# Last head and low-rank stage: row variance from a Gram matrix, and one output chunk through ScalarE and GpSimd

## What is computed

```python
Bx = jnp.einsum('bni,bri->bnr', x, B[adapter_ids])      # rank 16
out = jnp.einsum('bnr,bor->bno', Bx, A[adapter_ids])    # back to 512
mu = jnp.mean(out, -1); var = jnp.mean(jnp.square(out - mu), -1)
h = (out - mu) * jax.lax.rsqrt(var + EPS) * gamma + beta
h = dyn_quant_linear(h, w1, b1); h = gelu(h); h = dyn_quant_linear(h, w3, b3)
x = x + h
```

## Time and profile before

| | us |
|---|---|
| median of 3 runs | 570.07 (569.52 to 570.65) |
| the profiled execution, its own time | 569.7 |
| span of that execution in the trace | 567.9 |
| TensorE busy | 542.2 |
| VectorE busy | 485.0 |
| ScalarE busy | 363.0 |
| GpSimd busy | 400.2 |

### The profile page before, as it was taken

One profiled execution on the slowest core, in us unless ns is written; L12 is line 12 of the kernel. 1 busy time (PEld: TensorE's weight loads), 2 busy tenths in 40 slices (PEclk: granted clock), 3 DMA queues, 4 the chain that ended last, 5 costly groups with the idle time before them and its releaser, 6 DMA issues.

```text
span 567.9 us, 10485 instructions
## 1 busy us (share of the span) xinstructions
PE 542.2 (95%) x3135; PEld 425.0 (75%) x3139; DVE 485.0 (85%) x626; ACT 363.0 (64%) x940; POOL 400.2 (70%) x410
## 2 busy tenths in 40 slices
PE   6999989999999999999999999999999999987885
PEld 3555768888888888888888888888888888865432
DVE  3553859997999799979997999799979998976897
ACT  3573567657665766576657665766576656665895
POOL 3005577799779977997799779977997799851063
PEclk9999999999999999999999999999999999999999
DMA  8752435422442244124512451245124312200003
GB/s 289 180 123 76 123 88 160 113 56 58 137 124 51 62 133 126 43 65 133 128 37 66 134 132 33 61 136 136 34 61 135 97 34 61 80 1 1 1 20 129
DMA packets 38172, 51.93 MB, mean 91 GB/s; under 512 B 12100, under 2 KB 20452, under 8 KB 38148
## 3 DMA queue, kind: packets, MB, share of 16 engines
q1 hardware_dynamic: 35652, 46.94, 31.3%
q10 hardware_dynamic: 2016, 3.48, 1.9%
q0 software_dynamic: 480, 1.22, 0.7%
HBM read 28.55 MB, written 2.10 MB: 54 GB/s over the span
## 4 chain that ended last, share of the span: by engine, by line
PE 80%; DVE 10%; issue 3%; DMA 2%; ACT 2%; POOL 2%; ACTq 0%; SPq 0%; DVEq 0%; POOLq 0%
PE pair L1378 23%; PE pair L1379 23%; PE flow L1367 9%; PE flow L1494 9%; PE flow L1486 4%; PE pair L1315 4%; DVE y_max L1191 2%; DVE raw_v L1081 1%; PE flow L1372 1%; DMA stage<-in_x 1%; PE flow L1315 1%; DMA swap_q<-raw_q 1%; DVE rope_c L1203 1%; DVE ctx_lo L1102 1%; DVE probs L1203 1%
## 5 line engine op out<-in xcount | busy, mean ns | idle before, releaser
L1095 DVE SCALAR_TENSOR_TENSOR accT<-pair,so_now,accT 128x1024 f32<-128x1024 f32 x125 | 157.2, 1274 | 14.8 <-PE pair L1379 13.9
L1081 DVE SCALAR_TENSOR_TENSOR raw_q<-pair,sc_now,raw_q 128x1024 f32<-128x1024 f32 x90 | 115.4, 1283 | 6.2 <-ACT raw_q L777 2.8
L560 POOL TENSOR_TENSOR probs<-probs,rowinv 128x512 f32<-128x512 f32 x64 | 66.8, 1044 | 65.4 <-DVE rowinv L1068 65.4
L722 ACT ACTIVATE probs<-flow,negmax 128x128 f32<-128x128 f32 x248 | 87.6, 369 | 32.8 <-DVE negmax L1049 32.8
L1378 PE MATMUL pair<-ctx_hi,wo 128*128 128x512 f32 x256 | 104.9, 410 | 2.8 <-issue 1.5
L1378 PE MATMUL pair<-h_hi,wq 128*128 128x512 f32 x240 | 100.0, 417 | 0.3 <-ACT raw_q L777 0.3
L1379 PE MATMUL pair<-ctx_lo,wo 128*128 128x512 f32 x256 | 100.2, 392 | 0.0
L1379 PE MATMUL pair<-h_lo,wq 128*128 128x512 f32 x240 | 94.1, 392 | 0.0
L529 POOL TENSOR_TENSOR rope_s<-swap_q,consts 128x512 f32<-128x512 f32 x62 | 80.2, 1293 | 9.2 <-DMA swap_q<-raw_q 9.2
L541 POOL TENSOR_TENSOR qT<-rope_c,rope_s 128x512 f32<-128x512 f32 x62 | 79.3, 1280 | 4.4
L529 POOL TENSOR_TENSOR rope_c<-raw_q,consts 128x512 f32<-128x512 f32 x62 | 78.8, 1293 | 0.0
(11 more groups left out here) (242 smaller groups left out, 966.3 us busy)
## 6 DMA issues: line engine op xcount, KB each, us to landing
swap_q<-raw_q SPq DMA_DIRECT2D x62, 256.0 KB, 3.7
wq_i<-in_L_attn_qw_q SPq DMA_DIRECT2D x8, 1024.0 KB, 5.6
wo_i<-in_L_attn_qw_o SPq DMA_DIRECT2D x32, 256.0 KB, 2.6
swap_k<-raw_k SPq DMA_DIRECT2D x14, 256.0 KB, 3.6
wkv_i<-in_L_attn_qw_k SPq DMA_DIRECT2D x8, 256.0 KB, 3.7
wkv_i<-in_L_attn_qw_v SPq DMA_DIRECT2D x8, 256.0 KB, 4.0
stage<-in_x ACTq DMA_DIRECT2D x4, 256.0 KB, 5.7
probs<-in_L_ffn_w ACTq DMA_DIRECT2D x4, 256.0 KB, 8.2
```

The source lines that it names most:

```text
L560: pool.tensor_tensor(pr, pr, rowinv[:, f, :].unsqueeze(2).broadcast_to([P, HB, P]), ALU.mult).then_inc(probs_done, 1)
L722: e = act.activation(probs[:, 0, f, seq(b)], bank[:, seq(b)], ACT.Exp, bias=negmax[:, f, b:b + 1], accum_out=rowsum[:, f, b:b + 1])
L1081: dve.scalar_tensor_tensor(out=into, in0=flat(pair[pair_of(h, (kind, j), last)][:, :, :]), scalar=sc_now[:, scale_slot(kind, h), j:j + 1], ...
L1095: dve.scalar_tensor_tensor(out=a, in0=flat(pair[pair_of(h, (O, c), last)][:, :, :]), scalar=so_now[:, (h if c == 0 else h - 1) % 2, c:c + ...
```

## The change

The A factor is loaded as it is into a tile of its own, low_nat, and is no longer turned early. In the last group TensorE sums it at h = 2 with a matmul by ones and VectorE subtracts the mean (`centre_factor`). At h = 3 TensorE makes its Gram matrix (`gram_factor`) and turns it (`turn_factor`); VectorE keeps the Gram matrix with a block mask (`keep_gram`) and makes low_gT from the turned factor and gamma (`scale_factor`). The variance comes from low_gram times low_h (one product of 128x256), a product with low_h on VectorE (low_m), and two small matmuls with the strip mask (`sum_squares`). The eight products L1583 and the statistics on both engines go.

Chunk 2 of head 31's output isn't drained by VectorE any more: ScalarE scales it into tail_o (memory of raw_q), and GpSimd adds tail_o to accT[:, 2, :]. The low-rank product is linear, so TensorE takes the two parts apart: `low_rows(2, accT[:, 2, :])` before head 31's output(0), and `low_rows(2, tail_o)` in the tail. Of the four b3 additions, VectorE takes chunk 0, ScalarE the other three, chunk 2 last, after GpSimd.

```diff
-                sp.dma_start(nA[:, :, b * R:(b + 1) * R],
+                sp.dma_start(low_nat[:, :, b * R:(b + 1) * R],
...
 (GpSimd, behind its loop)
-            pool.wait_ge(d_rows, 64)
-            pool.wait_ge(low_centred, 1)
-            pool.tensor_tensor(low_gT[:, :], low_aT[:, :], rows[:, 0, :], ALU.mult).then_inc(low_scaled, 1)
             pool.tensor_copy(ident_h[:, :], ident).then_inc(half_made, 1)
+            pool.wait_ge(tail_kept, 1)
+            pool.wait_ge(lowh_done, LOWH_BY[2])
+            pool.tensor_tensor(accT[:, 2, :], accT[:, 2, :], tail_o, ALU.add).then_inc(tail_added, 1)
...
 (ScalarE: the early copy, and behind its loop)
-            act.wait_ge(lowT_done, 2)
-            act.activation(low_aT[:, :], banks[6], ACT.Copy).then_inc(lowT_kept, 1)
...
-            act.wait_ge(low_summed, 1)
-            act.activation(low_sum[:, 1:2], low_sum[:, 0:1], ACT.Copy, scale=-1.0 / D).then_inc(low_mean, 1)
-            act.wait_ge(low_mean, 1)
-            act.activation(low_aT[:, :], low_aT[:, :], ACT.Identity, bias=low_sum[:, 1:2]).then_inc(low_centred, 1)
             act.activation(std[:, 0:1], ident[:, 0:1], ACT.Sqrt).then_inc(table_set, 1)
...
+            act.wait_ge(step_done, STEPS_LOOP + 2)
+            act.activation(tail_o, flat(pair[TAIL_PAIR[2]][:, :, :]), ACT.Copy, scale=so_now[:, (NH - 1) % 2, 2:3]).then_inc(tail_kept, 1)
             act.wait_ge(d_rows, 64)
-            for c in range(C):
-                act.wait_ge(lowh_done, HB * (c + 1))
-                act.activation(accT[:, c, :], accT[:, c, :], ACT.Identity, bias=b3_col[:, c:c + 1]).then_inc(b3_added, 1)
-            for k in range(HB, B):
-                act.wait_ge(low_done, k + 1)
-                act.activation((rope_c, rope_s)[k % 2][:, k // 2 % 2, :], banks[LOW_ORDER[k]], ACT.Square, accum_out=squares[:, k - HB:k - HB + 1]).then_inc(squares_done, 1)
+            add_b3(1)
+            add_b3(3)
+            add_b3(2)
...
 (VectorE)
+            def centre_factor():
+
+                dve.wait_ge(low_summed, 1)
+                dve.scalar_tensor_tensor(out=low_nat[:, :, :], in0=banks[4][:, 0:P].unsqueeze(1).broadcast_to([P, C, P]), scalar=-1.0 / D,
+                                         in1=low_nat[:, :, :], op0=ALU.mult, op1=ALU.add).then_inc(low_centred, 1)
...
+            def scale_factor():
+                dve.wait_ge(d_rows, 64)
+                dve.wait_ge(low_turned, 1)
+                dve.tensor_tensor(low_gT[:, :], banks[5], rows[:, 0, :], ALU.mult).then_inc(low_scaled, 1)
...
+                    if last and h == 2:
+                        centre_factor()
+                    if last and h == 3:
+                        keep_gram()
+                        scale_factor()
                     split_context(0)
...
-                    if last and h == 0:
-                        dve.tensor_reduce(low_sum[:, 0:1], low_aT[:, :], AX.X, ALU.add).then_inc(low_summed, 1)
...
-            for i, c in enumerate(range(1, C)):
-                dve.wait_ge(step_done, STEPS_LOOP + i + 1)
+            for c in (1, 3):
+                dve.wait_ge(step_done, STEPS_LOOP + c)
...
+            dve.wait_ge(lowh_done, LOWH_BY[0])
+            dve.tensor_scalar(accT[:, 0, :], accT[:, 0, :], b3_col[:, 0:1], None, ALU.add).then_inc(b3_added, 1)
...
-            dve.wait_ge(lowh_done, HB * C)
+            dve.wait_ge(lowh_done, LOWH_ALL)
             dve.tensor_tensor(low_h.rearrange("p (j n) -> p j n", j=2), flow[0][:, 0:2 * P].rearrange("p (j n) -> p j n", j=2),
                               parity.unsqueeze(2).broadcast_to([P, 2, P]), ALU.mult).then_inc(lowh_kept, 1)
...
+            dve.wait_ge(lowm_done, 1)
+            dve.tensor_tensor(low_m, banks[7][:, 0:2 * P], low_h, ALU.mult).then_inc(lowm_kept, 1)
+            dve.wait_ge(squares_done, 2)
+            dve.tensor_scalar(var[:, :], banks[7][:, 2 * P:2 * P + B], 0.0, EPS, ALU.max, ALU.add).then_inc(var_done, 1)
...
 (TensorE, last group)
                     if last and h >= 2:
+                        if h == 3:
+                            gram_factor()
                         output(2)
+                        if h == 2:
+                            pe.wait_ge(dve_drained, drains_by(g, 1, (O, 3), first, last))
+                            sum_factor()
+                        if h == 3:
+                            turn_factor()
                         output(3)
...
                     context(1)
+                    if last and h == 3:
+                        pe.wait_ge(ctx_split, 2 * n + 1)
+                        pe.wait_ge(dve_drained, drains_by(g, h, (O, 3), first, last))
+                        low_rows(2, accT[:, 2, :], first=True)
...
 (TensorE, behind the tail's steps)
+            low_rows(0, accT[:, 0, :])
+            pe.wait_ge(dve_drained, DRAINS_LOOP + 1)
+            low_rows(1, accT[:, 1, :])
+            pe.wait_ge(tail_kept, 1)
+            low_rows(2, tail_o)
+            pe.wait_ge(dve_drained, DRAINS_LOOP + 2)
+            low_rows(3, accT[:, 3, :], last=True)
+            pe.wait_ge(gram_kept, 1)
             pe.wait_ge(lowh_kept, 1)
-            pe.wait_ge(low_centred, 1)
-            for b in LOW_ORDER:
-                pe.matmul(banks[b], low_h[STRIPS[b // 2], seq(b % 2)], low_aT[STRIPS[b // 2], :],
-                          start=True, stop=True).then_inc(low_done, 1)
+            pe.matmul(banks[7][:, 0:2 * P], low_gram[:, :], low_h, start=True, stop=True).then_inc(lowm_done, 1)
...
-            pe.wait_ge(low_scaled, 1)
-            for b in range(HB):
-                pe.wait_ge(stats_done, b + 1)
-                scaled_product(b)
+            scaled_product(0)
+            scaled_product(1)
+            sum_squares()
+            scaled_product(2)
+            scaled_product(3)
```

More of the change, by code:

```diff
@@ L146, in build @@
         k_turned = probs[:, 1, :, :]
-        low_h = kT[:, 0:2 * P]
+        low_h, low_m = kT[:, 0:2 * P], kT[:, 2 * P:4 * P]
+        tail_o = raw_q[:, :, :].rearrange("p f n -> p (f n)")
         q_flat = qT[:, :, :].rearrange("p a (b i) -> p (a b) i", i=D)
@@ L1429, in _ @@
             early_wide(V, 3, V_PAIRS[3])
-            pe.wait_ge(exp_done, 1)
-            for c in range(C):
-                mm = pe.transpose(banks[6][:, seq(c)], nA[:, c, :], ident)
-            mm.then_inc(lowT_done, 1)
             pe.wait_ge(lowT_kept, 1)
@@ L1513, in scores_ahead @@
                         elif last and h == 2:
-                            pe.wait_ge(dve_drained, drains_by(g, 1, (O, 3), first, last))
+                            pe.wait_ge(low_centred, 1)
                         else:
```

108 lines of the change are left out of this document (67 added, 41 removed).

## The result

| | median, us | lowest to highest | runs |
|---|---|---|---|
| kernel before, beside it | 569.41 | 568.72 to 570.65 | 11 |
| changed kernel | 571.76 | 568.83 to 572.94 | 11 |

The changed kernel takes 1.0033 of the time before (95% interval 1.0021 to 1.0044). It is slower by 0.33%, where I forecast 568.1 us and 0.87 for faster. The profiled execution is the quickest of the eleven, with 568.83 us (span 567.0, mean granted clock 0.995); six of the others had a mean clock of 0.99 and took 571.8 to 572.9. This spread is the first thing to see: of 79 executions of the kernel before, timed beside the later experiments, 65 had a clock of 0.998 or more (median 568.93 us) and 14 one of 0.995 to 0.997 (median 570.24), none less. By this measure the kernel before loses its clock too, but seldom and for short; where, no trace shows.

A forecast was written before the change was run, and what follows sets the result against it. TensorE's pace was taken to bound the kernel until 521 us, then one serial chain to norm(0), with VectorE busy behind it. Norm(0) 2.1 us earlier, plus 0.15 lost behind, made -2.0 from 570.07: 568.1 us, range 566.3 to 569.1.

The forecast's parts named there:

- The sum: Whole kernel: 2.1 us gained up to norm(0), 0.15 us lost behind it, -2.0 us in all, giving 568.1 us.
- the rival that says otherwise: Tail, 522 to 527 us: TensorE under 3 us busy, clock falls to 1.2 GHz, 571 us or more; chance 0.04.
- the comparison with 4 to 8 us: Argument against a clock fall: TensorE busy 2.13 of 4 us there, yet the clock was 1.00.
- the eight matmuls L1644 remain: Argument against a clock fall: these matmuls stay in the changed kernel.
- The point of decision: Feed-forward stage: a clock fall decides at about 2 us lost, a sixth of the stage.
- The b3 addition waits for GpSimd: Tail, before low_h: VectorE's addition waits for GpSimd's to end, 1.4 us, low_h at 524.8 instead of 523.4.
- the row of the cast: Early cast L1001: 0.56 us against 0.23 for L951's same shape, ending just behind GpSimd's L478; taken as showing the wait.
- The Gram route: Tail, low_h to norm(0): variance by the Gram matrix, low_h ending at 525.2, norm(0) at 528.6, 2.1 us earlier.
- The additions in the last heads: Heads 30 and 31: added work hidden in idle time except four transposes before output(3), +0.22 us on the path.
- Behind norm(0): Feed-forward stage: TensorE's remaining products push the second residual turn and ScalarE's queue, +0.15 us.
- The range: Measured time: from just under the no-wait-for-GpSimd case to the edge of the gain-given-back case, 566.3 to 569.1.

The follow-up runs named there:

- late: Changed kernel with VectorE's b3 addition of chunk 0 moved from ahead of low_h to behind low_m; 566.53 us, 0.9950 of the kernel before.
- fill4: Changed kernel with four matmuls that nobody reads in TensorE's wait for low_h; 567.78 us, 0.9979 of the kernel before.
- gram: Changed kernel with chunk 2 drained by VectorE again and all four b3 additions on ScalarE; 567.73 us, 0.9983 of the kernel before.
- gap: Kernel before with one VectorE instruction on unused data (128x1024) added ahead of low_h; 569.9 us, 1.0011 of the kernel before.

## Why the prediction was wrong, point by point

**The clock was taken as full: the step that failed.** The sum assumed that TensorE keeps 2.4 GHz, and the rival that says otherwise got 0.04. The clock falls in 28 of 31 executions of the changed kernel, and for long in 21 of them (clock at most 0.993, median 571.72 us); the three at 1.00 have 568.09, the seven at 0.995 have 568.83. The rival's place was right, and its figures were near: TensorE busy under 3 us from 522 to 527 (3.20 measured), and 571 us or more (571.76 in the first runs, 570.63 and 570.61 in the repeats). Two reasons for the low chance were wrong. The first was the comparison with 4 to 8 us, where TensorE was busy 2.13 of 4 us at a clock of 1.00. It compares busy shares. Two more rows of the kernel before, TensorE in order of time, give the longest idle stretch of those 4 us, 0.96, and the one that the changed kernel's 1.80 takes the place of, 0.62:

```profile
4.90 0.63 PE L1268 MATMUL pair<-consts,stage 128*128 128x128 f32 x4 [0.96 <-DMA stage<-in_x]
...
524.55 0.71 PE L1583 MATMUL pair<-low_aT,kT 32*128 32x512 f32 x3 [0.62 <-DVE kT L1153]
```

The sum itself had that number: low_rows(3) from 522.65, done near 523.3, and low_h from 524.8 to 525.2 leave TensorE idle for 1.9 us, where the earlier trace rows have low_h 0.78 us behind the start of the rows. I added 1.4 us to the chain and did not ask what TensorE does meanwhile. The second was "the eight matmuls L1644 remain": they stand behind the stretch and cannot prevent it. The point of decision, a sixth of the feed-forward stage at the low level, was also near: 3.4 us of low clock cost 1.6 us behind norm(0) (39.0 against 37.4), and about 10 us cost 4.8 by the two traces.

The Trainium skill, "TensorE: Matmul & The Clock Gate", section "What's actually happening", says that the throttled state is the default and that activity releases it, and that the chip's measure of activity does not start with the kernel, so that the transition varies from run to run. The traces agree with the last: the same instructions with the same wait of 1.77 to 1.80 us ran once at a mean clock of 1.00, once at 0.995 and once at 0.990. They fit the first in so far as the clock comes back while TensorE works without a pause (near 535.0, at the end of the idle matmuls L1708); no run here shows which state is the default.

**The b3 addition waits for GpSimd: right.** 2.10 us, ending 0.55 behind GpSimd's addition; 0.74 us with no GpSimd beside it (late). Forecast 2.2 and 0.6. On the path it costs 1.1 us, forecast 1.4; GpSimd's addition is 2.38 us, not 2.54, and begins 0.41 us behind the last step, as forecast (0.42). The Trainium skill's rule from "SBUF — State Buffer", section "Who interferes with whom", which speaks against this place for the addition, holds here; it was the row of the cast that I had gone by, and both gave the same. What neither said is that the wait is paid twice, the second time as a longer idle stretch of TensorE.

**The Gram route: right in sum.** Last step to norm(0) was forecast at 7.37 us (528.6 - 521.23) and is 7.48. The parts are off against each other: low_h starts 3.26 behind the last step (forecast 3.57), and from low_h to norm(0) it is 4.22 (forecast 3.8). The second comes from TensorE's queue: the matmuls with four columns start 1.81 behind low_h's end (524.18 to 525.99; forecast 1.5, from 525.2 to 526.7), since the Gram product ahead of them starts 0.15 behind low_h's end, where nothing was set, and holds the array for 0.60 (524.33 to 524.93), where 0.43 was set. They take 0.61 us where 0.5 was set. low_m is ready at 525.53, before they start, so VectorE doesn't hold them up.

**The additions in the last heads: right in sum, wrong in the parts.** One more row of the kernel before, and then the changed kernel's TensorE at head 31:

```profile
509.13 0.39 PE L1379 MATMUL pair<-ctx_lo,wo 128*128 128x512 f32 x1
```

```profile
508.37 0.39 PE L1401 MATMUL pair<-ctx_lo,wo 128*128 128x512 f32 x1
...
508.60 1.05 PE L1470 MATMUL pair<-low_nat 128*128 128x128 f32 x8
...
509.41 0.47 PE L1400 MATMUL pair<-ctx_hi,wo 128*128 128x512 f32 x1
...
510.42 0.60 PE L1476 MATMUL pair<-consts,low_nat 128*128 128x128 f32 x4
...
510.77 0.48 PE L1400 MATMUL pair<-ctx_hi,wo 128*128 128x512 f32 x1
```

The Gram matrix's four matmuls in fp32 are eight instructions and hold the array for 0.81 us (508.60 to 509.41), where I took 0.45 from transposes, which are one instruction each. They stand where a wait for a drain was, and output(2) follows with no idle: from output(1)'s last matmul to output(2) it is 1.04 us (508.37 to 509.41), before 0.90 (509.13 to 510.03), so 0.14 lies on the path. The transposes hold the array for 0.35 where I took 0.45, and 0.23 of that had been free, so they add 0.12. In one piece it is 2.40 us from output(1)'s last matmul to output(3), before 2.16 (511.29 - 509.13): 0.24 us, and the forecast was 0.22. Whether it reaches the end I can't tell: the last output step's end moves by 1.6 us between three traces of this one kernel (520.44 to 522.04). VectorE's parts were hidden, as forecast: 0.28 and 0.68 us with 0.83 of idle left before the next split.

**Behind norm(0): right at full clock.** 37.4 us against 37.2, forecast 37.2 + 0.15. At full clock the forecast gain stands: fill, which is the changed kernel with nothing else but the wait filled, gains 2.1 us (569.25 to 567.17), and the forecast was 2.0. The changed kernel's own three executions at 1.00 are too few to say it as well: they lie 0.6, 2.1 and 2.3 us below the kernel before's median in their rounds.

**The range** (566.3 to 569.1) followed from the chances and fell with them. A case that is decided by the clock needed a price on the high side with its own weight: by the counts above about two thirds of the executions.

**What stays open**: what exactly the clock answers to, how long a wait may be before it is at risk, and what share the thin work behind it has. With the wait filled no execution was under 0.998 (0 of 17); with waits of 0.71 to 0.83 us it was 3 of 10 (fill4), 4 of 12 (gram), 2 of 5 (late) and 2 of 12 (gap), with 1.8 us 28 of 31. But the kernel before, which has a wait of 1.46 us at 517.12, had 14 of 79. So the length of one wait isn't the whole condition. What sets these apart was not tried.

## What to carry to other kernels

Where a change lengthens a chain between two engines, write down how long TensorE stands idle in one piece there, before and after, and not only its busy share over a window: here 0.62 us became 1.80, and with that wait filled the same change gained what its sum had said, to 0.1 us. It is a warning and no rule: 1.46 us elsewhere in the kernel before did less. A VectorE addition from SBUF to SBUF like b3's belongs where GpSimd is idle or where nobody waits behind it; moving one line by two instructions was worth 1.1 us, and took 1.1 us off the idle stretch too. Fill what is left of a wait with as many idle matmuls as fit in it and no more: behind the moved addition three did what eight did, without holding up the product behind them, while four in the full 1.8 us were too few in 3 of 10 executions.

## What the runs showed of the hardware

- With the same program and the same wait on TensorE (1.77, 1.79 and 1.80 us) the granted clock fell for about 10 us, not at all, and for 3.4 us. It also fell for 3.4 us behind a wait of 0.71 us (late), after 2.8 us of TensorE work without a pause. The mean clock of an execution sorts its time: 571.72 us at 0.993 and below, 568.83 at 0.995, 568.09 at 1.00 (21, 7 and 3 executions of the changed kernel).
- At 1.2 GHz eight matmuls of 512 bf16 columns take 3.61 us (1.89 at full clock), and two fp32 products of 32 rows by 512 columns (four instructions) 2.07 (1.13).
- A TENSOR_SCALAR of 128x1024 in fp32 on VectorE takes 0.74 us alone and 2.10 when it is issued 0.83 us into a 2.38 us addition on GpSimd. It then ends 0.55 us behind GpSimd's, which is less than its whole 0.74. VectorE's drain, which reads PSUM, kept its 1.28 us beside the same addition (520.55 to 521.83).
